# Fused graph attention on one core: how the running segment maxima get from rows to columns and back

## The reference, cut to what matters

```python
e = leaky_relu(alpha_s[src] + alpha_d[dst], 0.2)
m = segment_max(e, dst, num_segments=N)
ex = exp(e - m[dst])
s = segment_sum(ex, dst, num_segments=N)
alpha = ex / (s[dst] + 1e-16)
out = segment_sum(h[src] * alpha[:, :, None], dst, num_segments=N)
```

## Time and profile before

| what | value |
|---|---|
| runs, median of 3 | 8620.68 us |
| profiled execution, own time | 8664.63 us |
| its span | 8662.7 us |
| mean granted TensorE clock | 0.821 |
| busy: PE, DVE, ACT, POOL | 5621.8, 4989.0, 3877.8, 5844.0 us |
| changed function, pass 0a, from first gather | 981 to about 2440 us |
| pass 0b | 2559 to about 3991 us |
| last pass | 7283 to about 8614 us |

### The profile page before, as it was taken

One profiled execution on the slowest core, in us unless ns is written; L12 is line 12 of the kernel. 1 busy time (PEld: TensorE's weight loads), 2 busy tenths in 40 slices (PEclk: granted clock), 3 DMA queues, 4 the chain that ended last, 5 costly groups with the idle time before them and its releaser, 6 DMA issues. The chain is left out here.

```text
span 8662.7 us, 136659 instructions
## 1 busy us (share of the span) xinstructions
PE 5621.8 (65%) x25128; PEld 3980.1 (46%) x25129; DVE 4989.0 (58%) x11551; ACT 3877.8 (45%) x9075; POOL 5844.0 (67%) x8186
## 2 busy tenths in 40 slices
PE   6442367667646666773677777748787763667765
PEld 5441244444424444442555555535555542444444
DVE  6445255556545555553777887754444444566666
ACT  2230255555424555552344444425555542555554
POOL 0556677777747777775466776757777765888884
PEclk9999687887767888776889998968888875788887
DMA  4111333333313333330466666523333322334442
GB/s 145 50 51 41 83 101 101 100 100 101 86 45 102 101 101 101 101 101 21 139 172 173 185 176 173 145 62 100 102 101 101 102 74 81 106 105 109 107 108 76
DMA packets 582372, 894.76 MB, mean 103 GB/s; under 512 B 308788, under 2 KB 359137, under 8 KB 581877
## 3 DMA queue, kind: packets, MB, share of 16 engines
q0 software_dynamic: 245984, 649.30, 27.5%
q1 hardware_dynamic: 335876, 218.84, 9.3%
q10 hardware_dynamic: 416, 25.60, 0.9%
HBM read 859.36 MB, written 59.47 MB: 106 GB/s over the span
## 5 line engine op out<-in xcount | busy, mean ns | idle before, releaser
L2024 POOL DMA_INDIRECT ad_ring<-tab_qv,ad_idx x808 | 768.8, 951 | 496.8 <-issue 242.1
L2440 POOL DMA_INDIRECT ae_ring<-tab_a,ae_idx x808 | 777.9, 963 | 399.4 <-PE ae_po L2597 199.9
L1520 POOL DMA_INDIRECT at_ring_0a<-tab_s,at_idx_0a x808 | 771.1, 954 | 368.6 <-DVE at_rows_0a L1577 207.3
L1520 POOL DMA_INDIRECT at_ring_0b<-tab_s,at_idx_0b x808 | 772.4, 956 | 349.8 <-DVE at_rows_0b L1577 174.1
L1520 POOL DMA_INDIRECT at_ring<-tab_s,at_idx x808 | 781.3, 967 | 272.8 <-issue 119.0
L2590 PE MATMUL ae_pM<-ae_we,ae_featT 64*128 64x256 f32 x1616 | 501.8, 461 | 211.2 <-issue 169.2
L1700 PE MATMUL at_po_0a<-at_rows_0a,at_hot_0a 128*128 128x264 f32 x1616 | 559.5, 504 | 101.1 <-DVE at_begin_0a L111 28.4
L1700 PE MATMUL at_po_0b<-at_rows_0b,at_hot_0b 128*128 128x264 f32 x1616 | 551.5, 499 | 110.7 <-DVE at_begin_0b L111 32.7
L1700 PE MATMUL at_po<-at_rows,at_hot 128*128 128x260 f32 x1616 | 540.9, 492 | 111.8 <-DVE at_begin L111 27.0
L2218 PE MATMUL ad_pk<-node_a,ad_hr 128*128 x1616 | 459.9, 433 | 210.7 <-DVE ad_prod L2101 107.7
L565 POOL DMA_INDIRECT recs_s<-rnk_recs_now,rnk_pos_now x294 | 288.3, 981 | 400.7 <-DVE rnk_both L465 178.2
(11 more groups left out here) (538 smaller groups left out, 14649.4 us busy)
## 6 DMA issues: line engine op xcount, KB each, us to landing
at_rr_0a<-relrow_d SPq DMA_DIRECT2D x102, 256.0 KB
at_rr_0b<-relrow_d SPq DMA_DIRECT2D x102, 256.0 KB
ad_rr<-relrow_d SPq DMA_DIRECT2D x102, 256.0 KB
at_rr<-relrow_s SPq DMA_DIRECT2D x102, 256.0 KB
ae_feat<-attr_pad SPq DMA_DIRECT2D x808, 32.0 KB
rnk_lrow<-lorow_f SPq DMA_DIRECT2D x98, 256.0 KB
attr_pad<-in_edge_attr_dram ACTq DMA_DIRECT2D x1, 25000.0 KB, 79.3
at_ring_0a<-tab_s,at_idx_0a POOLq DMA_INDIRECT x808
```

What stands on the lines that cost most here:

```text
L1520: eng.indirect_dma_start(out=ring[:, t.slot * STEP + u, :], out_offset=None, in_=table, in_offset=bass.IndirectOffsetOnAxis(ap=idx[:, t.sl ...
L2024: eng.indirect_dma_start(out=ring[:, t.slot * STEP + u, :], out_offset=None, in_=table, in_offset=bass.IndirectOffsetOnAxis(ap=idx[:, t.sl ...
L2440: eng.indirect_dma_start(out=ring[:, k, :], out_offset=None, in_=table, in_offset=bass.IndirectOffsetOnAxis(ap=idx[:, k:k + 1], axis=0))\
```

## The change

VectorE turns the maxima with its own 32 x 32 block transposes in SBUF, and the whole of the maximum, `y` to `shrink`, comes ahead of `rows1` and all additions. The scan `fwd` now writes its row reversed, so that its last value lies in column 0. The line buffers have 64 rows, of which rows 0 and 32 count (two heads each), with 2 x 17 values; the totals are loaded into those two rows, and the separate load of the last total is gone. On TensorE the four trips and the 8 fillers after trip 2 are gone; `back_turned` comes before `reduce(3)` and waits for `rows3`, since it overwrites the weights that `rows3` reads. SyncE waits once for two fills before the first masks.

```diff
-        V = (["rescale", "rows0"] + scored + ["rows1", "add0", "add1", "add2", "add3", "col1", "carried", "carry",
-             "add4", "add5", "add6", "add7", "rows2", "begin", "full", "bwd", "rows3",
-             "add8", "add9", "add10", "add11", "col2", "back"] + under
-             + ["add12", "add13", "add14", "add15", "factor"])
+        V = (["rescale", "rows0"] + scored + ["turn1", "carried", "turn2", "full", "bwd", "turn3", "back", "turn4", "carry"] + under
+             + ["rows1", "add0", "add1", "add2", "add3", "rows2", "add4", "add5", "add6", "add7", "rows3",
+                "add8", "add9", "add10", "add11", "add12", "add13", "add14", "add15", "factor"])
...
-            totf = sb(f"at_totf_{tag}", [1, BUFS, H, STEP], F32, c)
+            totf = sb(f"at_totf_{tag}", [R, BUFS, 2, STEP + 1], F32, c)
...
-                        eng.dma_start(tot_last[:, t.slot:t.slot + 1], od["totals"][0:1, bass.ds(t.n * STEP + STEP - 1, 1)])\
-                            .then_inc(masks_in[t.slot], 16)
...
+                    eng.wait_ge(blank, 2)
                     feed_masks(Turn(0, 0))
...
-                            v.did("fwd", eng.tensor_tensor_scan(fwd[:, :], brk, tops_in, -BIG, ALU.add, ALU.max))
...
+                            v.did("fwd", eng.tensor_tensor_scan(fwd[:, ::-1], brk, tops_in, -BIG, ALU.add, ALU.max))
+                            done("fwd", t)
+                            v.did("turn1", eng.transpose(line_f[:, :, 1:STEP + 1], fwd[:, 0:SQUARE].rearrange("r (h u) -> r h u", h=2)))
+                            done("turn1", t)
                             v.did("carried", eng.tensor_tensor_scan(line(run_f[:, :, :]), line(totf[:, t.slot, :, :]),
                                                                     line(line_f[:, :, :]), -BIG, ALU.add, ALU.max))
                             done("carried", t)
...
+                            v.did("turn2", eng.transpose(begin[:, :].rearrange("r (h u) -> r h u", h=2), run_f[:, :, 0:STEP]))
+                            done("turn2", t)
                             v.did("full", eng.tensor_tensor_scan(full[:, :], brk, tops_in, begin[:, 0:1], ALU.add, ALU.max))
                             done("full", t)
                             v.did("bwd", eng.tensor_tensor_scan(bwd[:, ::-1], brk_after, full[:, ::-1], -BIG,
                                                                 ALU.add, ALU.max))
...
+                            done("bwd", t)
+                            v.did("turn3", eng.transpose(line_b[:, :, 0:STEP], bwd[:, 0:SQUARE].rearrange("r (h u) -> r h u", h=2)))
+                            done("turn3", t)
...
+                            done("back", t)
+                            v.did("turn4", eng.transpose(end[:, :].rearrange("r (h u) -> r h u", h=2), run_b[:, :, 1:STEP + 1]))
+                            v.did("carry", copy(eng, line_f[:, :, 0:1], run_f[:, :, STEP:STEP + 1]))
+                            done("turn4", t)
...
+                        weigh_rows(1)
+                        add(0, 1, 2, 3)
+                        weigh_rows(2)
+                        add(4, 5, 6, 7)
+                        weigh_rows(3)
+                        add(8, 9, 10, 11)
                         add(12, 13, 14, 15)
...
                         reduce(0)
-                        trip(1, "fwd", row1, fwd[:, P - 1:P], R)
                         reduce(1)
-                        trip(2, "carry", col2, line(run_f[:, :, :]), 1)
-                        if scores:
-                            keep_busy(eng, spare, 8)
                         reduce(2)
-                        trip(3, "bwd", row3, bwd[:, 0:1], R)
...
                         spread(0, gs)
-                        trip(4, "back", col4, line(run_b[:, :, :]), 1)
-                        reduce(3)
                         if scores:
+                            if sums:
+                                eng.wait_ge(vec, v.at(f"rows{quads - 1}", t))
                             eng.wait_ge(act, s.at("exp", t))
...
+                        reduce(3)
                         spread(1, gs)
```

More of the change, by code:

```diff
@@ L51 @@
 LN_EPS = 1e-5
+SQUARE = 32
 assert TAIL == 2 and T % UC == 0 and TR <= P and E % P == 32 and TURNS == LAPS * BUFS
@@ L1622, in step @@
                             done("carried", t)
-                            v.did("carry", eng.scalar_tensor_tensor(
-                                out=line_f[:, :, 0], in0=run_f[:, :, STEP - 1], scalar=tot_last[:, t.slot:t.slot + 1],
-                                in1=row1_h[:, :, STEP - 1], op0=ALU.add, op1=ALU.max))
-                        else:
-                            v.skip("col1", "carried", "carry")
-                        add(4, 5, 6, 7)
-                        weigh_rows(2)
-                        if scores:
-                            eng.wait_ge(mat, m.at("trip2", t))
-                            v.did("begin", copy(eng, begin[:, :], col2))
-                            done("begin", t)
+                            v.did("turn2", eng.transpose(begin[:, :].rearrange("r (h u) -> r h u", h=2), run_f[:, :, 0:STEP]))
+                            done("turn2", t)
                             v.did("full", eng.tensor_tensor_scan(full[:, :], brk, tops_in, begin[:, 0:1], ALU.add, ALU.max))
@@ L1637, in step @@
                                                                 ALU.add, ALU.max))
-                        else:
-                            v.skip("begin", "full", "bwd")
-                        weigh_rows(3)
-                        add(8, 9, 10, 11)
-                        if scores:
-                            eng.wait_ge(mat, m.at("trip3", t))
-                            v.did("col2", copy(eng, line_b[:, :, 0:STEP - 1], row3_h[:, :, 1:STEP]))
-                            done("col2", t)
+                            done("bwd", t)
+                            v.did("turn3", eng.transpose(line_b[:, :, 0:STEP], bwd[:, 0:SQUARE].rearrange("r (h u) -> r h u", h=2)))
+                            done("turn3", t)
                             v.did("back", eng.tensor_tensor_scan(
@@ L1648, in step @@
                                 line(line_b[:, :, :])[:, ::-1], -BIG, ALU.add, ALU.max))
-                        else:
-                            v.skip("col2", "back")
-                        if scores:
-                            eng.wait_ge(mat, m.at("trip4", t))
-                            v.did("end", copy(eng, end[:, :], col4))
-                            done("end", t)
+                            done("back", t)
+                            v.did("turn4", eng.transpose(end[:, :].rearrange("r (h u) -> r h u", h=2), run_b[:, :, 1:STEP + 1]))
+                            v.did("carry", copy(eng, line_f[:, :, 0:1], run_f[:, :, STEP:STEP + 1]))
+                            done("turn4", t)
                             v.did("top", eng.tensor_tensor_scan(top[:, ::-1], brk_after, full[:, ::-1], end[:, 0:1],
@@ L1664, in step @@
                                                                   masks[:, t.slot, FIRST:FIRST + P], ALU.add))
-                            v.did("shrink", eng.tensor_scalar(less[:, EX:EX + 1], begin[:, :], top[:, 0:1], 0.0,
+                            v.did("shrink", eng.tensor_scalar(less[:, EX:EX + 1], begin[:, 0:1], top[:, 0:1], 0.0,
                                                               ALU.subtract, ALU.min))
                         else:
-                            v.skip(*under)
+                            v.skip(*scored, "turn1", "carried", "turn2", "full", "bwd", "turn3", "back", "turn4", "carry", *under)
+                        weigh_rows(1)
[4 more added lines that the diff above has]
+                        add(8, 9, 10, 11)
                         add(12, 13, 14, 15)
@@ L1702, in reduce @@
                                                            start=True, stop=True))
-                        def trip(k, after, out, of, size):
-                            if not scores:
-                                return m.skip(f"trip{k}")
-                            eng.wait_ge(vec, v.at(after, t))
-                            eng.sem_inc(told, 1)
-                            m.did(f"trip{k}", eng.transpose(out, of, ident[0:size, 0:size]))
                         def spread(h, gs):
```

50 lines of the change are left out of this document (19 added, 31 removed).

## The result

The change made the kernel slower. Median 8864.83 us of 4 runs (8840.32 to 8869.84) against 8624.8 us for the kernel before on the same chip (4 runs): ratio 1.0273, 95% interval 1.0249 to 1.0298. Forecast was 8223 us.

A forecast was written before the change was run, and what follows sets the result against it. The loop from `y` to the next `y` was taken as the bound: 14.65 + 1.0 + 9.2 = 24.85 us a turn, saving 160 + 145 + 95 = 400 us. 8664.6 - 400 = 8265, times 0.995: 8223 us; range 8070 to 8600.

The forecast's parts named there:

- The block of maxima: On VectorE, `y` to the end of `shrink`, with four transposes and other small steps: 5.7 us, range 5.0 to 7.3.
- The bound is the loop from `y` to the next `y`: In the three passes, this loop of 27.73 us, not GpSimd, was said to limit the kernel before.
- What follows `exp`: End of `exp` to next `y`, with `reduce(3)` now behind `back_turned`: 6.9 or 11.5 us, middle 9.2, against today's 7.8.
- GpSimd is a floor at 23.05 us, not the bound: Sixteen gathers 1.44 us apart need 23.05 us a turn, leaving GpSimd 4 to 5 us to spare.
- the rival's floor: Rival: quick releases give 20.9 us, so GpSimd binds at 23.05; 620 us saved, about 8005 us; chance 0.15.
- The vector path beside it ... needs about 3.3 us and hides: After `exp`, VectorE's `add15`, `factor`, `rescale`, `rows0` and `y` take about 3.3 us, hidden beside the other work.
- Late releases: TensorE's results assumed released up to some 4.5 us late while SyncE's row loads run; 1.0 us taken ahead of `exp`.
- The guess at the cause: TensorE's results were taken to come late while SyncE's 256 KB row loads run; why was left open.
- GpSimd's second quad waits for `rows1` ... but the gather has a turn in hand: GpSimd waits until 6.9 us; its turn ends about 25.0 us behind `y`, but `picked` wants the previous turn's ring.
- The fallen clock: Rival: TensorE's clock stays 0.5 throughout, turn 26.2 us, 205 us saved, about 8415 us; chance 0.15.
- The slower rival: `mm7` falls into the row load, `reduce(1)` 5.0 us, `reduce(3)` 6.6: turn 28.3 us, 110 us lost; chance 0.12.

The follow-up runs named there:

- u_after: The changed kernel itself, run again on a chip where the kernel before takes 7344.16 us: 7485.19 us, ratio 1.0194.
- s_bef_plain: The kernel before with plain transfers of fixed rows in place of GpSimd's gathers, leaving out the choice of rows by index: 6845.4 us, single run.
- d_norows: The changed kernel with SyncE's row loads cut from 128 partitions to 16, leaving out most rows the spreads need: 8877.19 us in one run.
- i_bef_spmove: The kernel before with SyncE's loads of rows, masks, totals and `nrel` moved behind ScalarE's `parts`: 8599.8 us, ratio 1.0029.
- b_rows1: The changed kernel with `rows1` moved ahead of the block of maxima, right behind `rows0`: 8743.41 us, ratio 1.0133.
- n_rows1: The changed kernel with `rows1` ahead of the block of maxima, on another chip where results are late: 8712.61 us, ratio 1.0156.
- e_spmove: The changed kernel with `rows1` ahead of the block and SyncE's loads moved behind ScalarE's `parts`: 7486.0 us, ratio 1.0203.
- a_fill: The changed kernel with the 8 filler matmuls put back behind `reduce(1)` on TensorE: 8963.63 us, ratio 1.0392.

## Why the prediction was wrong

Step by step, us behind `y` in pass 0b (medians, each taken by itself, so that they need not add up):

| step | forecast | before, late chip | after, late chip | u_after, prompt chip | s_bef_plain (before, no gathers, prompt chip) |
|---|---|---|---|---|---|
| `shrink` ends | 5.7 | 18.2 | 5.4 | 5.4 | 13.2 |
| `rows1` ends | 6.9 | 2.7 | 6.5 | 6.5 | 2.7 |
| `add4` starts (`mm4` is done) | not given | 4.8 | 8.9 | 8.9 | 4.8 |
| ScalarE's quad 3 starts | 9.0 or 10.3, and 1.0 for lateness | 7.2 | 10.6 | 10.8 | 5.9 |
| `exp` ends | 15.65 | 18.6 | 15.35 | 15.55 | 13.7 |
| `parts` starts | not given | 24.4 | 25.0 | 18.4 | 17.7 |
| `exp` end to next `y` | 9.2 | 7.8 | 12.4 | 8.0 | 7.0 |
| turn | 24.85 | 27.45 | 27.5 | 23.6 | 20.6 (mean 20.2) |

**The block of maxima** was right: four transposes at 0.20 us, 5.4 for 5.7. So was `exp`, within 0.3 us on either chip, its wait for `shrink` gone and `mm7` the last release before quad 3. (By the prediction's own terms `exp` ends at 13.8 or 15.1, not 14.0 or 15.3; that changes nothing.)

**The step that failed is the reading "The bound is the loop from `y` to the next `y`", 27.73 us taken for a chain of work that gets shorter when the trips go. In the sum the term is "What follows `exp`": 9.2 us, and 12.4 measured.** The gain ahead of `exp` came, 3.3 us (18.6 to 15.35; the prediction read 19.9 off a single turn), and the stretch behind it grew by 4.6 us (7.8 to 12.4): `parts` hardly moved, from 24.4 to 25.0. In the last pass, where the forecast missed by most (23.9 us against 28.7), it is the same: `exp` ends at 14.8 in place of 17.2, and the stretch behind it takes 13.8 in place of 8.3. What the 27.73 us hold besides work shows beside s_bef_plain, where nothing is late and no gather runs: there `shrink` ends at 13.2, not 18.2, and the turn is 20.2 us. `exp` waits for `shrink` there too, 2.9 us (median), but 5 of the 18 us ahead of it were not the trips. What stands above 20.2 in the kernel before differs by chip:

- On late chips it is the lateness of results, in turns of 26 to 28 us. "GpSimd is a floor at 23.05 us, not the bound" held there as far as the floor goes.
- On prompt chips it is most likely GpSimd. The kernel before has no trace there; its turn is worked out. The three windows of u_after average 24.06 us a turn, and before is 141 us, or 0.94 us a turn, faster: 23.1 us, which is GpSimd's 23.05. So there the rival's floor had been reached before the change, with some 3 us of slack under it.

**The change makes the chain longer**, by 3.4 us without gathers (20.2 to 23.6). On a prompt chip GpSimd's floor hides the larger part, and 0.94 us a turn is left; on a late chip this and the lateness can't be priced apart. Where the 3.4 us come from is read from the timelines and was not tested by a run of its own. The block puts all of its 5.4 us ahead of `rows1`, so `mm4` to `mm7` come 4 to 5 us later than before (`add4` starts at 8.9, not 4.8; `add7` at 11.1, not 5.8), at clock 0.50, after TensorE stood; how much of it the clock alone costs is not separated. `exp` ends 1.9 us later. And `add12` to `add15`, which in s_bef_plain run at 13.1 to 15.5, ahead of `alphas`, run at 17.1 to 18.9 behind it; `factor`, `rescale`, `rows0` and the register load of 3.4 us follow. **"The vector path beside it ... needs about 3.3 us and hides"** failed with that: from the start of `add15` to `y` it is 5.2 us, since the register load was left out of it, and on a prompt chip it sets the end. On a late chip it still hid.

**"Late releases"** was named as the largest unknown, and its size and place were wrong. It stood in the sum with 1.0 us ahead of `exp` and 2.3 behind it. Ahead of `exp` it was about zero; behind it, `parts` comes at 25.0 us behind `y` where nothing but the chip changed from 18.4. Of these 6.6 us 3.9 lengthen the turn (27.5 against 23.6). The guess at the cause, SyncE's loads, fell for size (d_norows) and for place (i_bef_spmove).

**"GpSimd's second quad waits for `rows1` ... but the gather has a turn in hand"** was half right. Its sum, a turn of GpSimd ending 25.0 us behind `y`, was good (24.4 in after). For the data it does have a turn in hand. But on late chips taking that wait away, with the rest of that edit, gave 1.4% (b_rows1) and 1.5% (n_rows1) of the time, half of the loss; on a prompt chip e_spmove, which has it away too, gained nothing (1.0203 against 1.0194 on another chip).

**The rivals.** The fallen clock came true (0.72); its price was not measured by itself, and a_fill, which raised the clock with fillers, cost time. The slower rival, 8730 us, had the right sign with the right half of its mechanism: the end behind `exp` was late (12.4 us, 11.5 in the rival), but `mm7` was not, and it decided on the wrong place.

**What stays open** is why results are late on some chips. The order of `reduce(3)`, the size of the row loads and the place of SyncE's loads are excluded there; so is the clock, since in pass 0b results are late in before at 0.78 and prompt in u_after at 0.80. GpSimd's gathers and memsets are the suspect: from the 1.45 us spacing, from `parts` following the last gather from after to b_rows1, and from the count that hardly rises during a memset on late chips. But i_bef_spmove shows the second only loosely, and the runs without gathers, with a shorter pause and without TensorE's register load all fell on chips where nothing is late. That GpSimd causes the lateness was not shown. Not tried either: `reduce(3)` ahead of `back_turned`, which the chain speaks for, on a prompt chip, and an earlier load of VectorE's registers. No version that ran beats the kernel before.

## What to carry to other kernels

Before a measured loop is shortened, find out how much of it is chain: replace the suspected floor by something cheap and look at the turn again. Here that one run (20.2 us on a prompt chip, where the trace, of a late one, showed 27.7) would have shown that much of the loop was not a chain that the change could shorten. Such a run tells most beside a trace of the same chip. Work that seems to hold up the chain may be hidden in its gaps; gathered in one piece on the busiest of its engines, it is exposed and delays everything queued behind it. And where a wait's named releaser makes no sense, treat the gap as unknown time that may stay, not as time to be saved.

## What the runs showed of the hardware

- The same kernel takes 8580 to 8625 us on some chips and 7332 to 7344 us on others, 17% apart, and within 0.6% of each other on either side. The gather takes 0.95 us on both, and DMA packets take as long (4160 bytes: 161 ns, median). What differs is when the count that TensorE raises goes up: up to 5 us behind the matmul's recorded end (which is modelled) against 0.1 in the turns shown, not early in the turn (`add4` to `add7` start within 0.3 us of each other on both kinds of chip), and hardly ever during one of GpSimd's memsets (4 to 6% of the rises in before and after, 22% in u_after). SyncE's issues from the first masks to the last totals take 3.2 us in after and 2.6 in u_after (medians of pass 0b). Phases that the change does not touch differ too: a pass of gathers elsewhere in the program, first to last, is 1385 us in after and 1201 in u_after.
- A load of 15 register values takes 3.4 us of VectorE's queue on either kind of chip, and the profile shows it only as idle time put down to another engine.
- VectorE's transpose of 64 x 32 f32 in blocks took 0.20 us. The Trainium skill (VectorE: DVE Perf Modes, The three transpose paths) gives 311 ns for a 128 x 128 bf16 tile, of which this is an eighth of the elements at twice the width; no run here shows that form.
